# More of the background's ticks beside the wide attention, fewer beside the experts' tile loop

## The reference

```python
# layer 0, attention: 16 heads of 16, causal, 32 largest scores of a row kept
scores = q @ k.T / 4;  masked = all but the 32 largest of a row -> -inf
x = x + ga * (softmax(masked) @ v @ Wo.T + bo)
# layer 0, feed-forward: one of 8 experts for each row
x = x + gb * relu(h @ We[e] + be[e]) * p
# layer 1, attention: 16 heads of 64, causal softmax          <- "wide" in the kernel
x = x + ga * (softmax(q @ k.T / 8 + mask) @ v @ W_out + b_out)
# layer 1, feed-forward: a block of its own, on z
z = z + attention16x16(layernorm(z))                         # <- "flip" in the kernel
z = z + sum over the 2 best of 8 experts of w * (gelu(z' @ w1) @ w2)   # <- "route" and "moe"
```

## Time and profile before

| | us |
|---|---|
| median of 3 runs (5928.27 to 5935.34) | 5930.14 |
| the profiled execution | 5932.03 |
| its span, first to last instruction | 5930.3 |

### The profile page before, as it was taken

One profiled execution on the slowest core, in us unless ns is written; L12 is line 12 of the kernel. 1 busy time (PEld: TensorE's weight loads), 2 busy tenths in 40 slices (PEclk: granted clock), 3 DMA queues, 4 the chain that ended last, 5 costly groups with the idle time before them and its releaser, 6 DMA issues. The chain is left out here.

```text
span 5930.3 us, 83316 instructions
## 1 busy us (share of the span) xinstructions
PE 4491.5 (76%) x30341; PEld 2890.1 (49%) x30341; DVE 4104.7 (69%) x8455; ACT 2753.8 (46%) x6035; POOL 1908.1 (32%) x1563
## 2 busy tenths in 40 slices
PE   4444478988677678988777688998777686999776
PEld 2333345666434454666533454666533453666334
DVE  6999957887787656888688656887778655222630
ACT  2444424666244533666345351666445360554333
POOL 2565512444323421444323430444333431000001
PEclk7656689999788889999888788999888797999888
DMA  3000000000301120000121121000031201000312
GB/s 124 11 12 25 1 22 25 18 13 15 57 12 63 48 96 22 15 16 18 36 33 35 69 76 48 13 13 13 15 54 32 75 30 50 16 10 10 63 63 72
DMA packets 113333, 213.59 MB, mean 36 GB/s; under 512 B 25728, under 2 KB 70632, under 8 KB 109552
## 3 DMA queue, kind: packets, MB, share of 16 engines
q1 hardware_dynamic: 104736, 190.94, 11.8%
q0 software_dynamic: 6144, 16.79, 0.9%
q10 hardware_dynamic: 2048, 0.53, 0.0%
HBM read 154.38 MB, written 49.73 MB: 34 GB/s over the span
## 5 line engine op out<-in xcount | busy, mean ns | idle before, releaser
L1492 DVE MAX8 vals<-work 128x8 f32<-128x128 f32 (+7 forms) x1536 | 1080.7, 743 | 0.4
L1866 POOL TENSOR_SCALAR keep<-ssb,vals 128x128 bf16<-128x128 f32 (+7 forms) x512 | 876.4, 1723 | 0.0
L469 PE MATMUL ring<-ident,pr 128*128 128x128 f32 x2304 | 490.9, 334 | 423.8 <-POOL pr L1871 372.2
L1506 DVE MATCH_REPLACE8 work<-vals,work 128x128 f32<-128x128 f32 (+7 forms) x1024 | 750.6, 739 | 0.0
L1853 POOL TENSOR_TENSOR pool_step<-ones 128x2 f32<-128x2 f32 x256 | 50.0, 195 | 2132.1 <-DVE vals L1492 2131.6
L576 PE MATMUL pA<-SC 128*128 128x512 f32 (+3 forms) x1536 | 615.6, 510 | 82.8 <-DVE SC L1635 42.3
L1871 POOL TENSOR_TENSOR pr<-keep,pr 128x128 f32<-128x128 bf16 (+7 forms) x512 | 649.0, 1289 | 0.0
L469 PEld LDWEIGHTS ring<-ident,pr 128*128 128x128 f32 x2304 | 334.8, 171 | 573.4 <-POOL pr L1871 395.5
L1143 ACT ACTIVATE prT<-ring 128x512 f32<-128x512 f32 (+1 forms) x768 | 380.5, 498 | 407.2 <-PE ring L469 405.8
L1621 DVE TENSOR_REDUCE nmax<-pA 128x1 f32<-128x1024 f32 (+7 forms) x512 | 384.4, 751 | 259.6 <-PE pA L577 248.0
L1492 DVE MAX8 vals<-ssb 128x8 f32<-128x128 f32 (+7 forms) x512 | 363.0, 750 | 263.7 <-ACT ssb L1131 246.8
(11 more groups left out here) (225 smaller groups left out, 7968.9 us busy)
## 6 DMA issues: line engine op xcount, KB each, us to landing
SC<-in_w SPq DMA_DIRECT2D x64, 512.0 KB, 7.3
stage<-parts SPq DMA_DIRECT2D x384, 64.0 KB, 2.4
parts<-SC SPq DMA_DIRECT2D x72, 256.0 KB, 2.5
SC<-parts SPq DMA_DIRECT2D x144, 128.0 KB, 7.9
SC<-in_wqkv SPq DMA_DIRECT2D x32, 384.0 KB, 2.9
rows_out<-SC SPq DMA_DIRECT2D x92, 128.0 KB, 1.7
SC<-rows_in SPq DMA_DIRECT2D x20, 512.0 KB, 3.9
SC<-in_ffn_we SPq DMA_DIRECT2D x4, 2048.0 KB, 10.3
```

Source lines behind the costliest of these rows:

```text
L469: mm = pe.transpose(r[:, blk % 4 * P:blk % 4 * P + P], pr0[:, p % 2, blk * P:blk * P + P], ident[:, :])
L1492: m = v.max(vals0[:, y, i, 8 * n:8 * n + 8], src[:, lo:hi])
L1506: done[i] = cht.mark(v.match_replace(out=work0[:, lo:hi], in_to_replace=vals0[:, y, i, 8 * n:8 * n + 8], in_values=src[:, lo:hi], imm_valu ...
L1866: pool.tensor_scalar(keep0[:, lo:hi], ssb0[:, p % 2, lo:hi], vals0[:, p % 2, i, TOPK - 1:TOPK], None, ALU.is_ge).then_inc(s["k"], 1)
```

## The change

Two shares in `Pace.STAGES` are altered. No instruction is added or removed on any engine; what changes is where in the streams the ticks stand.

```diff
-    STAGES = (("wide", 8 * 17, 0.51), ("prep", 12, 0.04), ("flip", 8 + 48, 0.22), ("route", 6, 0.04),
-              ("moe", 23, 0.19))
+    STAGES = (("wide", 8 * 17, 0.56), ("prep", 12, 0.04), ("flip", 8 + 48, 0.22), ("route", 6, 0.04),
+              ("moe", 23, 0.14))
```

## The result

The changed kernel takes 5965.49 us (median of 4, 5963.54 to 5971.6) against 5930.11: a ratio of **1.0058, 95% interval 1.0044 to 1.0071**. It is slower by 35 us where 38 us of gain were forecast, and lies outside the range. The profiled execution has a span of 5963.8 us.

A forecast was written before the change was run, and what follows sets the result against it. Wide was taken as bound by PE with short stalls on ACT, moe by the chain from PE to ACT and back. Terms of -25 + 19.5 - 7 - 3 + 2.8 = -12.7 us, three sequences -38, gave 5892; range 5862 to 5934.

The forecast's parts named there:

- Moe, -25: In moe, 25 full ticks leave at 0.95 us each, four of eight exponentials with them: 25 us less a sequence.
- Prep, -7: In prep, the second half projection no longer waits behind a spread and values: 7 us less, bounds -9 and 0.
- the select at row tile 6: In prep, POOL's select 286 falls before the norm's reciprocal roots; one tick and a reciprocal less make up: 0.
- Route, +2.8: In route, two selects ahead of the last four scatters delay the rows' load and the loop: 2.8 us more.
- Flip, -3: In flip, one tick less (-1.1), a lighter end (-5), a spread moved inside (+3): together 3 us less.
- the spread then falls at point 42 ... +3: In flip, the spread moves from the end to a stretch where PE and ACT are busy: 3 us more.
- Wide, +19.5: In wide, 25 more ticks at about 0.70 us (17.5) and one spread of 1.95 us: 19.5 us more.
- DVE, though busy, isn't what the others wait for: In wide, ACT's wait for DVE's row maxima is 44.7 us with the background, 40.5 without; PE bounds the stage.
- The first rival: DVE becomes the bound of wide: an added tick costs 1.76 us, 5971 us in all; chance 0.12.
- the turning point of 1.3 us a tick: In wide, the price of an added tick from which the whole kernel turns slower than before: about 1.3 us.
- The second rival: The ends of prep and flip give nothing, 10 us go: -2.7 a sequence, 5922 us; chance 0.18.
- the third: Wide takes ticks at PE's work alone (11.5 + 2), moe gives 30: -23.7 a sequence, 5859 us; chance 0.10.

The follow-up runs named there:

- e9: The kernel before, old shares, with two bf16 buffers in place of one f32 for the spread reciprocals: 5908.74 us, ratio 0.9962.
- e5: The changed kernel with two bf16 buffers in place of one f32 for the spread reciprocals, spreads where they were: 5905.72 us, ratio 0.9950.
- e13: The kernel before, old shares, with two buffers and DVE's MAX8 and MATCH_REPLACE8 on half of each tile's columns (another output): 5570.1 us.
- e14: The changed kernel with two buffers and DVE's MAX8 and MATCH_REPLACE8 on half of each tile's columns (another output): 5532.77 us.
- e15: The kernel before with only three shares altered, wide 0.61, flip 0.12, moe 0.19: 5860.57 us, ratio 0.9881.

## Why the prediction was wrong

Each term in us for one sequence, as a mean of the three with the background: as forecast, as measured, with two buffers in both kernels, and with half of DVE's background work besides.

| | wide | prep | flip | route | moe | sum |
|---|---|---|---|---|---|---|
| forecast | +19.5 | -7 | -3 | +2.8 | -25 | -12.7 |
| before to after | +32.0 | -9.1 | +10.1 | +3.9 | -25.7 | +11.3 |
| e9 to e5 | +28.3 | -8.4 | +5.7 | +2.1 | -25.7 | +2.0 |
| e13 to e14 | +10.2 | -6.4 | +8.7 | +2.1 | -27.0 | -12.3 |

(These are the profiled executions. By the medians e5 is 3 us under e9 in all, where these rows make it 6 above.)

*Moe, -25:* right; -22.5, -27.3, -27.3. Four pairs of table loads left. By the 2.66 us a switch of the Trainium skill, page "ScalarE: Activation LUTs", section "What ACT_TABLE_LOAD costs", moe would have given 36 if all of it were on the path, and it didn't; by the row (1.30 us from load to exponential) it comes out.

*Prep, -7:* right in mechanism and size (-9). The second half projection starts 0.6 us after the first ends, and no cost of the select at row tile 6 shows.

*Route, +2.8:* right in mechanism (load issued behind two selects, loop released by the DMA); 4.6, 2.4 and 4.8 measured. PE's idle time right before the loop is 3.4 us and not 8, because its ticks had themselves waited for a select until 2014.44.

*Flip, -3:* the step that failed is "the spread then falls at point 42 ... +3". I had the chain before me, 4.05 us of ACT's wait for POOL, and counted its removal from flip's end but not its length elsewhere. The length depends on how far the `select` queued ahead has got when ACT's first copy is done: in the old kernel it had run for 3.4 us, here it hadn't begun, and the wait was 8 us. Without the wait in either kernel flip still grows by 5.7 us on average, so the wait is 4 of the 13 us between forecast and result. The other 9 stay open. In the first sequence the granted clock in flip is 0.81 in place of 0.84, and from e9 to e5 it goes from 0.84 to 0.80 with PE busy for 6 us more on the same work, as much as flip grows there; but from e13 to e14 PE is busy for 3 us more and flip grows by 8.4. That last pair also shows that it isn't DVE's load.

*Wide, +19.5:* the term is mis-sized by 12.5 us. Some 4 of them are the wait behind the select, since the spread that moved in was priced at its 2 us of matrix products alone. The rest is the price of the ticks: 24 to 31 us for 25 where neither kernel has the wait, up to twice the mean, for a reason that I had ruled out: "DVE, though busy, isn't what the others wait for". I had read this off the level of ACT's wait for the row maxima, with and without the background, and left out PE's wait for L1635. But a chain that goes round PE, DVE and ACT in turn shows each engine waiting a little for another, and the level of a wait, 8 us more with 251 ticks than with none, says little of what the next tick will cost. Its growth over the next 25 ticks did tell, and halving DVE's part showed whose the price was. There is a slip in the sum besides: PE's 0.46 us and twice the 0.17 of stalls are 0.80 us a tick, not 0.70, which would have made the term +22 and the forecast 5899.

The first rival, DVE as the bound of wide, had the right engine and the wrong limit: DVE is busy for 81% of wide in the changed kernel and for 86% in e15, so 80% wasn't its ceiling. Its price of 1.76 us a tick was too high (0.9 to 1.26 without the select's wait), as was the turning point of 1.3 us a tick, which is 1.2 by its own terms. That its total of 5971 was near 5965 is luck: its wide was 14 us a sequence too long, and flip's error, which it shared, filled the difference.

A rule of the Trainium skill bears on this. The page "Trainium Kernel Development and Optimization", section "Performance Expectations", says that a matrix product's busy time is a bad metric, because matmuls are pipelined, and that the busy share of the weight loads is a good one. I argued with PE busy for 89% of wide. By the weight loads, PE is at 260.95 / 408.8 = 64% alone, at 348.3 / 565.7 = 62% with 251 ticks and at 360.47 / 599.5 = 60% in the changed kernel, while in e13 and e14 it is 63.4% and 63.6%. So PE was less full with the background than without, and the more ticks, the less. The trace is in line with the rule but doesn't decide for it: PE's busy share tells the same, 95% alone, 89% and 87% with the ticks and 91 to 92% in e13 and e14. What was missing was the comparison between windows, by either share.

The second rival (the ends give nothing) and the third (wide at PE's own work) fell: the ends gave what was forecast, and wide's price went the other way. With DVE's work halved, though, wide did take the ticks at about PE's own work.

## What to carry to other kernels

The mean price of background work in a stage says little of the next piece's: take it from a run with a little more and a little less, look at which waits grew between the two, and where a loop passes through several engines, halve one engine's part to learn whose the price is. Correct a change's effect by the same repair in both kernels: two buffers took 10.7 us off the changed kernel's wide, but they took 8.3 off the old one's too. When work is moved by a schedule, look for the pieces that hold a wait across two queues (here a one-buffer hand-over from ACT to POOL with a long instruction ahead on POOL), because where these fall can outweigh everything else: 22 us in one place and 60 in another. At the old shares the stage that pays most for a tick was flip, at 1.35 us and still 1.2 for the next 24; taking ticks from there (49 of them) and not from moe made the kernel 1.2% faster by an edit of the same kind.

## What had not been expected of the hardware

The second half projection's neighbour, the first one in prep, ran slower in the changed kernel. Its 16 products took 7.08 us in the old kernel (start 1557.21) and 9.34 in the changed one, after PE had been idle for 21 us in both:

```profile
1584.94 3.67 PE L421 MATMUL ring<-ident,SC 128*128 128x128 f32 x16 [21.24 <-DVE SC L1418]
1589.40 9.34 PE L435 MATMUL pA<-hT,SC 128*128 128x512 f32 x16 [0.78 <-ACT hT L1097]
```

In the old kernel background transposes and scores stood between L421 and L435; in the changed one there are none. The windows of the projection alone, in the old kernel and in the changed one (PE, PEld, DVE, ACT, POOL, then the granted clock, DMA):

```profile
1557.21:1564.30 7.09, 7.09 (x19) 3.05 (x17) 0.00 (x0) 1.90 (x3) 4.37 (x3) 1.00 0.00 0
```

```profile
1589.40:1598.74 9.34, 9.34 (x19) 4.04 (x20) 0.00 (x0) 2.29 (x3) 0.00 (x0) 0.76 0.01 2
```

From PE's first transpose behind the idle stretch to the start of the projection the granted clock is 0.50 in both kernels, the lower of the two levels (1.2 GHz), and that takes 4.5 us in both (1552.68 to 1557.21, 1584.94 to 1589.40). In the old kernel PE works without a break in it, and the clock is at the upper level from about 1557.1, so that the projection runs wholly at it. In the changed kernel PE stands still for 0.78 us right before the projection, and the first 4.5 us of the projection are still at 0.50; the upper level comes at about 1593.9. The second sequence shows the same (7.21 and 9.33 us for the products, 0.98 and 0.76 over them). So the 2.3 us are the clock's; whether the short stop or the missing background work put off its rise was not tried.
